# A selective-scan kernel: the D skip as accumulating transposes, the state copies on ScalarE, the gate on VectorE

## The reference

```python
xi = silu(conv(x @ in_proj_x));  z = x @ in_proj_z
dt, B, C = split(xi @ x_proj);   dt = softplus(dt @ dt_w + dt_b)
h[t] = exp(dt[t] * A) * h[t-1] + dt[t] * xi[t] * B[t]     # per channel and state
y[t] = sum over states of h[t] * C[t]
y    = (y + xi * D) * silu(z)
out  = y @ out_proj
```

## Time and profile before

| what | value |
|---|---|
| median of 3 runs | 5188.53 us (5188.35 to 5191.7) |
| the profiled execution: own time, span | 5190.08 us, 5188.0 us |
| Mamba loop, first scan to last | 162 to 3766 us |
| busy in the span: PE, DVE, ACT, POOL | 4402.9, 4073.9, 3191.4, 3548.5 us |
| busy between 160 and 3766 us: DVE, POOL, PE, ACT | 3545.0, 3438.7, 2967.1, 2551.0 us of 3606 |

### The profile page before, as it was taken

The page is one execution under the profiler, slowest core; times in us unless marked ns, Lnnn a source line. Parts: engine busy times, 40 slices in busy tenths (PEclk is TensorE's granted clock), DMA queues, the critical chain, the costliest instruction groups (busy, mean ns, idle before and its releaser), DMA issues. The chain is left out here.

```text
span 5188.0 us, 70665 instructions
## 1 busy us (share of the span) xinstructions
PE 4402.9 (85%) x22602; PEld 3147.1 (61%) x22602; DVE 4073.9 (79%) x4200; ACT 3191.4 (62%) x4771; POOL 3548.5 (68%) x2133
## 2 busy tenths in 40 slices
PE   3888888888888888888888888888679999999999
PEld 1455555555555555555555555555558888888887
DVE  4799999999999999999999999999933333333332
ACT  4767676776767777777677677767534443444343
POOL 5899999999999999999999999999910000000000
PEclk7899999999999999999999999999889999999999
DMA  4533232333223322232222223222230000000000
GB/s 144 184 115 101 99 106 98 115 103 103 100 99 105 104 103 100 105 111 103 105 94 102 107 104 112 102 104 94 81 114 17 9 17 9 17 9 17 9 17 9
DMA packets 152610, 433.73 MB, mean 84 GB/s; under 512 B 12352, under 2 KB 96704, under 8 KB 117568
## 3 DMA queue, kind: packets, MB, share of 16 engines
q1 hardware_dynamic: 151296, 416.96, 23.0%
q10 hardware_dynamic: 896, 11.54, 0.6%
HBM read 384.42 MB, written 55.57 MB: 85 GB/s over the span
## 5 line engine op out<-in xcount | busy, mean ns | idle before, releaser
L1011 POOL TENSOR_TENSOR m_dBx<-m_u,m_Bs 128x1024 f32<-128x1024 f32 x1024 | 2410.9, 2368 | 36.6 <-DVE m_h L1174 30.1
L1174 DVE TENSOR_TENSOR_SCAN m_h<-bank,m_state,m_dBx 128x512 f32<-128x512 f32 x1792 | 2192.0, 1263 | 46.4 <-ACT bank L895 43.7
L895 ACT ACTIVATE bank<-m_dt,cols 128x512 f32<-128x512 f32 x2048 | 1385.3, 690 | 869.3 <-DVE m_h L1174 848.0
L715 PEld LDWEIGHTS bank<-ident,m_h 128*128 128x128 f32 x8192 | 1019.5, 147 | 509.4 <-issue 358.2
L715 PE MATMUL bank<-ident,m_h 128*128 128x128 f32 x8192 | 1251.9, 283 | 81.6 <-DVE m_h L1183 68.8
L1183 DVE TENSOR_TENSOR m_h<-m_h,bank 128x1024 f32<-128x1024 f32 x896 | 1069.1, 1193 | 7.6 <-PE bank L697 7.5
L697 PE MATMUL bank<-ident,m_Ct 128*128 128x128 f32 x3584 | 596.4, 291 | 543.4 <-DVE m_h L1183 538.1
L697 PEld LDWEIGHTS bank<-ident,m_Ct 128*128 128x128 f32 x3584 | 396.5, 141 | 1041.6 <-DVE m_h L1183 928.1
L1446 POOL TENSOR_TENSOR mv<-mv,norm_c 128x4 f32<-128x4 f32 x16 | 3.2, 202 | 1226.9 <-DVE mv L1464 1226.9
L602 PE MATMUL bank<-m_hT,m_w_in 128*128 128x512 f32 x1024 | 545.8, 619 | 20.3 <-ACT m_hT L776 20.2
L602 PE MATMUL bank<-m_xpre,m_diag 128*128 128x512 f32 x1024 | 529.6, 602 | 0.0
(11 more groups left out here) (123 smaller groups left out, 5005.9 us busy)
## 6 DMA issues: line engine op xcount, KB each, us to landing
m_Bs<-b_dram SPq DMA_DIRECT2D x256, 1024.0 KB, 4.7
m_Cs<-c_dram SPq DMA_DIRECT2D x128, 256.0 KB, 4.5
m_xy<-in_x SPq DMA_DIRECT2D x16, 512.0 KB, 7.2
xn_dram<-m_xn SPq DMA_DIRECT2D x16, 512.0 KB, 6.9
x_dram<-m_base SPq DMA_DIRECT2D x16, 512.0 KB, 7.1
yb_dram<-m_ysb SPq DMA_DIRECT2D x16, 512.0 KB, 7.8
m_xn<-xn_dram SPq DMA_DIRECT2D x16, 512.0 KB, 3.8
m_xy<-yb_dram SPq DMA_DIRECT2D x16, 512.0 KB, 5.8
```

The costliest lines, as they stand in the source:

```text
L715: mm = pe.matmul(YB[b][:, o:o + P], h[:, k % NH, m, tok:tok + P], ident[:, :], start=(s == 0 and o == 0), stop=(s == DS - 1), is_transpose ...
L895: act.activation(DA[SLOT[k]][:, :], dt[:, ch.batch, m, :], ACT.Exp, scale=cols[:, ch.ps, col:col + 1]).then_inc(S["da"], 1)
L1011: pool.tensor_tensor(dBx[:, k % NDBX, :, :], u[:, ch.batch, m, :], Bs[:, k // BP % 2, k % BP, :].unsqueeze(1).broadcast_to((P, 2, T)), ALU ...
L1174: dve.tensor_tensor_scan(h[:, k % NH, m, flip(ch)], DA[SLOT[i]][:, flip(ch)], dBx[:, k % NDBX, m, flip(ch)], initial, ALU.mult, ALU.add).t ...
```

## The change

- The D skip moves: ScalarE computes xD = D * xi (`scale_skip`, new, at steps 14, 16, 18 and 20), and TensorE adds it to the sums in PSUM with 8 more accumulating transposes per half (`turn_skip`, new), behind the last `turn_h` of the half. The evacuation now waits for these (`y_turned`).
- `skip` on VectorE becomes `gate`: z = (turned sum in PSUM) * z. GpSimd's `gate` goes.
- `keep_state` goes from GpSimd to ScalarE, at steps 2, 6, 10 and so on to 62.
- `P_UNITS` has six units instead of four: 0, 6, 9, 14, 20, 25.
- The first pair of z's silus moves from step 14 to step 12.
- `xi` is held for one chunk instead of two, `acc` for one half instead of two; two more C rows are loaded per chunk, with the order of the loads on the SP queue changed.

```diff
-P_UNITS = (5, 10, 17, 21)
+P_UNITS = (0, 6, 9, 14, 20, 25)
...
-AT_XI, AT_ZS = (24, 24, 31, 31), (14, 14, 57, 57)
+AT_XI, AT_ZS = (24, 24, 31, 31), (12, 12, 57, 57)
...
-GATE_S = (28, 12)
+AT_XD = (14, 16, 18, 20)
...
@@ SP, body @@
                 load_b(ch, 2)
+                load_c(ch, 2)
                 load_b(ch, 3)
...
-                load_c(ch, 2)
+                load_c(ch, 3)
                 load_b(ch, 4)
+                load_c(ch, 4)
...
-                load_c(ch, 3)
                 load_b(ch, 5)
...
+                load_c(ch, 5)
...
@@ TensorE @@
+            def turn_skip(ch, half):
+                pe.wait_ge(S["skip"], ch.at(KI, 2 * half + 2))
+                for t in range(TS):
+                    for m in range(2):
+                        o = t % 2 * HW + m * P
+                        mm = pe.matmul(YB[t // 2][:, o:o + P], xD[:, 2 * half + m, t * P:(t + 1) * P], ident[:, :],
+                                       start=False, stop=True, is_transpose=True, skip_group_check=True)
+                mm.then_inc(S["y_turned"], 1)
...
                             turn_h(*done, b)
+                            if b == 1 and done[1] % DS == DS - 1:
+                                turn_skip(done[0], done[1] // DS)
...
@@ ScalarE @@
-                            wait(act, S["gate"], ch.at(2, -2))
+                            wait(act, S["u_ready"], ch.at(2, 0))
...
+            def scale_skip(ch, g):
+                for m in range(KI):
+                    if g == AT_XD[m]:
+                        if m == 0:
+                            act.wait_ge(S["xi"], ch.at(KI, KI))
+                            act.sem_inc(S["go"], 1)
+                            wait(act, S["y_turned"], ch.at(2, 0))
+                        col = COL_D + m
+                        act.activation(xD[:, m, :], xi[:, m, :], ACT.Copy, scale=cols[:, ch.ps, col:col + 1]
+                                       ).then_inc(S["skip"], 1)
+
+            def keep_state(ch, p):
+                k = 2 * p
+                act.wait_ge(S["scan"], ch.at(STEPS, 2 * k + 4))
+                act.copy(state[:, ch.batch, k:k + 2, :], h[:, k % NH:k % NH + 2, :, 0 if rev(ch) else T - 1]
+                         ).then_inc(S["save"], 1)
...
-                act.wait_ge(S["turned"], ch.at(NU, DS * (half + 1)))
+                act.wait_ge(S["y_turned"], ch.at(2, half + 1))
...
                     z_silu(ch, k)
+                    scale_skip(ch, k)
+                    if k % 4 == 2:
+                        old = unit(ch, (k - 6) // 2)
+                        if old:
+                            keep_state(old[0], old[1] // 2)
...
@@ GpSimd: gate and keep_state and their calls go @@
...
@@ VectorE @@
-            def skip(ch, g, m):
+            def gate(ch, g, m):
                 q = ch.batch
                 if g == AT_Y[m] + DVE_LAG:
-
+                    dve.wait_ge(S["z"], ch.at(KI, m + 1))
                     wait_filled(dve, ch, J_Y[m])
-                    dve.scalar_tensor_tensor(out=xi[:, q, m, :], in0=xi[:, q, m, :],
-                                             scalar=cols[:, ch.ps, COL_D + m:COL_D + m + 1],
-                                             in1=FB[BANK[J_Y[m]]][:, :],
-                                             op0=ALU.mult, op1=ALU.add).then_inc(drain[BANK[J_Y[m]]], 1)
+                    dve.tensor_tensor(z[:, q, m, :], FB[BANK[J_Y[m]]][:, :], z[:, q, m, :], ALU.mult
+                                      ).then_inc(drain[BANK[J_Y[m]]], 1)
```

More of the change, by code:

```diff
@@ L167 @@
     "sp_exp", "sp_ln", "dt_done", "u_ready", "b_st", "b_in0", "b_in1", "c_in0", "c_in1", "da", "dbx", "scan", "save",
-    "c_fill", "weigh_d", "weigh_p", "turned", "y_evac", "gate",
+    "c_fill", "weigh_d", "weigh_p", "turned", "skip", "y_turned", "y_evac",
     "y_out", "yb_in", "base_in", "base_out", "xn_in", "xn_out", "comb",
@@ L355, in mamba @@
         no_halo = sb("no_halo", [P, KI, HALO])
-        xi = sb("xi", [P, BATCH, KI, T])
+        xi = sb("xi", [P, KI, T])
+        xD = sb("xD", [P, KI, T])
         z = sb("z", [P, BATCH, KI, T])
@@ L647, in front @@
                         pe.wait_ge(S["xi"], ch.at(KI, m + 1))
-                        part(ch, J_B, m, KI, w_x[:, m, :], xi[:, q, m, :], B0 + 2 * DS)
+                        part(ch, J_B, m, KI, w_x[:, m, :], xi[:, m, :], B0 + 2 * DS)
                 if g == AT_C:
@@ L664, in turn_y @@
                     o = m % 2 * P
-                    turn(J_Y[m], lambda s: acc[:, half, s, o:o + P], ch)
+                    turn(J_Y[m], lambda s: acc[:, s, o:o + P], ch)
             def tail(ch, g):
@@ L677, in tail @@
                                     pe.wait_ge(S["w_out"], 16 * (ch.ps + 1))
-                                pe.wait_ge(S["gate"], ch.at(2, 2))
+                                wait_drained(pe, ch, J_Y[2])
                             wait_free(pe, ch, J_OUT[i])
@@ L715, in turn_h @@
                         mm = pe.matmul(YB[b][:, o:o + P], h[:, k % NH, m, tok:tok + P], ident[:, :],
-                                       start=(s == 0 and o == 0), stop=(s == DS - 1), is_transpose=True,
+                                       start=(s == 0 and o == 0), stop=False, is_transpose=True,
                                        skip_group_check=True)
@@ L747, in flush @@
                         turn_h(ch, NU + k - T_LAG, b)
+                turn_skip(ch, 1)
                 for g in range(STEPS):
@@ L829, in xi_silu @@
                         if m == 0:
-                            wait(act, S["gate"], ch.at(2, -2))
+                            wait(act, S["u_ready"], ch.at(2, 0))
                         wait_drained(act, ch, J_CONV[m])
-                        act.activation(xi[:, ch.batch, m, :], u[:, ch.batch, m, :], ACT.Silu).then_inc(S["xi"], 1)
+                        act.activation(xi[:, m, :], u[:, ch.batch, m, :], ACT.Silu).then_inc(S["xi"], 1)
+            def scale_skip(ch, g):
[13 more added lines that the diff above has]
+                         ).then_inc(S["save"], 1)
             def z_silu(ch, g):
@@ L842, in evacuate @@
             def evacuate(ch, half):
-                if has(ch, -1):
-                    wait_filled(act, ch.go(-1), J_Y[2 * half])
+                before = (ch, 0) if half else (ch.go(-1), 2) if has(ch, -1) else None
+                if before:
+                    wait_filled(act, before[0], J_Y[before[1]])
                     act.sem_inc(S["go"], 1)
-                    wait_filled(act, ch.go(-1), J_Y[2 * half + 1])
+                    wait_filled(act, before[0], J_Y[before[1] + 1])
                     act.sem_inc(S["go"], 1)
-                act.wait_ge(S["turned"], ch.at(NU, DS * (half + 1)))
+                act.wait_ge(S["y_turned"], ch.at(2, half + 1))
                 for b in range(2):
-                    act.copy(acc[:, half, 2 * b:2 * b + 2, :], YB[b][:, :].rearrange("p (t n) -> p t n", t=2)
+                    act.copy(acc[:, 2 * b:2 * b + 2, :], YB[b][:, :].rearrange("p (t n) -> p t n", t=2)
                              ).then_inc(S["y_evac"], 1)
@@ L982, in make_u @@
                 pool.wait_ge(S["dt_done"], ch.at(2, half + 1))
[L983 to L1000, removed]
+                pool.tensor_tensor(u[:, q, m, :], dt[:, q, m, :], xi[:, m, :], ALU.mult).then_inc(S["u_ready"], 1)
             def weigh_b(ch, k):
@@ L1062, in body @@
                     weigh_b(ch, k)
[L1063 to L1066, removed]
                     old = unit(ch, k - W_LAG)
@@ L1077, in body @@
                         add_dt(ch.go(1), 0)
[L1078 to L1081, removed]
                     if joins(ch, -2):
@@ L1191, in body @@
                             for i in (2, 3):
-                                skip(ch.go(-1), g, i)
+                                gate(ch.go(-1), g, i)
                         for i in range(2):
-                            skip(ch, g, i)
+                            gate(ch, g, i)
                     old = unit(ch, k - W_LAG)
```

6 lines of the change are left out of this document (2 added, 4 removed).

## The result

The changed kernel takes 5216.49 us (median of 5 runs, 5214.68 to 5218.46), the kernel before 5188.53 on the same chip (5 runs, 5187.05 to 5191.7). The ratio is 1.0053, with a 95% interval of 1.0038 to 1.0068. The forecast was no change, 5184, with a range of 5130 to 5230 that holds the result; on the main point, that the time would stay, the forecast was wrong.

The account below looks back on a forecast made before the run. VectorE, 98% busy in the Mamba loop, was taken as the bound. Its saved work and the changed waits summed to about 0.0 us per chunk; with first chunk and tail about -5 us, 5188.5 became 5184, range 5130 to 5230.

Parts of the forecast that it names:

- VectorE's work: Two C products fewer and four cheaper skips per chunk: -2.34 us per chunk, -75 us in all.
- the four spots: Steps 13, 25, 32 and 44 of a chunk, where ScalarE is late or nearly late for VectorE's scans.
- Scan 13: VectorE waits for ScalarE's decay behind the evacuation and the silus of z: +2.6 us per chunk.
- Scans 25, 32 and 44: VectorE's waits change per chunk by +0.6 us at scan 25, -0.6 at scan 32, -0.2 at scan 44.
- The first chunk and the tail: The first chunk, with no evacuation at step 11, gains 2 us; the tail after the last scan changes by -1.5.
- GpSimd's work: GpSimd's work per chunk falls by 3.1 us; its lead over VectorE shrinks but holds, so nothing was added.
- the rival of a dry GpSimd: GpSimd runs dry by 1 us or more per chunk, so VectorE waits for `dBx`: 5216 us, chance 0.05.
- Silus hidden: Rival: z's silus on ScalarE cost VectorE nothing, so the work alone counts: 5112 us, chance 0.17.
- the block of 5.15 us: On ScalarE, one decay, the silus of z with two table loads, and the next decay: 5.15 us from start to end.
- Slow transposes: Rival: TensorE's skip transposes cost 283 ns each rather than 110, delaying both evacuations: 5271 us, chance 0.14.
- Table switches: Rival: ScalarE's four D scalings each switch activation tables, 10.3 us per chunk: 5387 us, chance 0.04.
- the longer drain: Skill page's drain of about 1.38 us per ScalarE table switch; step 13 would wait 2.8 longer, some 5270; no chance given.

Follow-up runs that it names:

- run 1: The changed kernel with z's first silus back at step 14 and the D scalings at steps 16, 18, 20, 22: 5168.65 us.
- run 7: The changed kernel without the D skip on any engine (no D scalings, no skip transposes; y lacks D * xi): 5150.73 us.
- run 4: The changed kernel with GpSimd's old four units (5, 10, 17, 21) and the C loads to match: 5253.88 us.
- run 6: The changed kernel with the 512 KB load of x moved behind the third B load of the chunk: 5209.19 us.
- run 3: The kernel before the change, with only the 16 state copies per chunk moved to ScalarE: 5204.52 us.
- run 9: The changed kernel with the 128x4 variance step moved from VectorE to ScalarE, at its step 57: 5201.65 us.
- run 5: The changed kernel with the 128x4 variance step as scalar_tensor_tensor, epsilon from a tile, in place of tensor_scalar: 5215.61 us.

## Why the prediction was wrong

**VectorE's work and the four spots: right.** -75 was -78.5; the gate took 662 ns rather than 692. Scan 13 was +2.6 and waited 2.55, by the very mechanism (run 1 takes it away, run 7 takes 0.87 of it). Scans 25, 32 and 44 came as 0.57, none and 0.34, against 0.6, none and 0.45; run 4 gives the first two back with the units. Only scan 44 was mis-sized, -11.2 us in the place of -6, in the kernel's favour. Together the terms that the sum had come out at -12 us in the place of -3. The first chunk and the tail, -3.5 together, came as -5 behind the last scan and up to +3 ahead.

**The step that failed is the sum itself, at "GpSimd's work": "I take nothing".** I asked only whether VectorE would wait for `dBx`. It hardly does, 2.9 us in the loop: the rival of a dry GpSimd named 5216, nearly the measured time, but by a mechanism that is not there. Nor does it save the forecast that the result lies in its range: it lies there since -12 us of walked terms offset 40 us of terms that the sum didn't have. Two costs hang on when GpSimd works, a third stands at the pass switch, and none had a term:
- The loop's ends, +14.7: GpSimd's product for unit 25 comes at its unit 29, its last `dBx` is later, the burst of loads is later by as much, and the code behind it. Shown by run 6, which takes the whole of it away, by run 4, in which they are at 11.4 us with GpSimd's old units, and by run 3, which clears the longer code. I had walked one chunk and not the jump between two; the waits of 1 to 1.5 were in the trace of before, and the 1.4 of the earlier trace rows is one of them.
- The variance step, +17.7: shown by runs 3, 4 and 9 for its price, by runs 4 and 5 for what it waits on. Its 0.52 before was already three times its length beside an idle GpSimd.
- The pass switch, +7.5: first a wait of 3.1 for TensorE, then two gaps of issue (1.1 and 2.2), then 1.7 at scan 13. TensorE stands for 3.47 us there, and from 1873 to 1880 us its granted clock is 0.54, near its lower level of 1.2 GHz (0.98 in the 13 us ahead of that): the eight transposes of the skip, 1.04 us long in nearly every other group, take 1.92. It goes with the old units (run 4), and no run took it by itself. What starts it stays open. The rows of TensorE after:

```profile
1873.31 1.12 PE L719 MATMUL bank<-ident,m_h 128*128 128x128 f32 x4 [3.47 <-DVE m_h L1195]
1876.78 1.92 PE L731 MATMUL bank<-ident,m_xD 128*128 128x128 f32 x8
```

The Trainium skill, "SBUF — State Buffer" (SBUF: two separate sides), says that VectorE and GpSimd share a pair of ports by an exclusive lock, held for a whole instruction, for which VectorE asks in a two-port mode or with two SBUF inputs. The trace agrees with the page: both forms of the step end 0.02 to 0.03 us behind GpSimd's product, and the scans, the C products and the statistics steps, which have at most one SBUF tensor as input, don't wait. The second form has two SBUF inputs; whether the first runs in a two-port mode no run shows. I had not weighed it, since so small a step did not seem to matter.

**The rivals.** Silus hidden (5112): no, but at step 14 they nearly are, in the first pass; the block of 5.15 us must start two steps later. Slow transposes (5271): refuted by run 7, and by the 0.87 of the eight in the trace. Table switches (5387): no load stands by the scalings. The load of 1.28 is again followed by its activation 1.29 behind its start (1082.01 and 1083.30), so the longer drain that the prediction cites shows in neither trace.

**Chances.** Slower had 0.33, and of it only 0.05 for GpSimd. A part for what the one chunk could not show, the loop's ends and small steps of VectorE beside a fuller GpSimd, belonged in the sum: 10 ends at up to 2.4 (the growth now seen at one jump) and 15 steps at up to one product of 2.37 would have given a bound of +60.

## What to carry to other kernels

When an engine off the path is given other work, walk everything that is timed by it: the loads that its progress releases, what is queued behind these (code too, at a loop's jump), and every small step of the bound engine that runs beside it. Walk the jump between iterations as well as one iteration. When the consumer of a buffer moves, the order of the queue that fills it must move too.

## What was unexpected of the hardware

- A 128x4 step of VectorE, in two forms with all tensors in SBUF, takes 0.16 to 0.17 us beside an idle GpSimd, 1.42 when it comes early into a GpSimd product of 2.37, and up to 3.78. A statistics step as small keeps its 0.14 to 0.18.
- After a loop's jump ScalarE gets its code only when the data burst ahead of it is nearly through: a gap of 6.97 us where 2.1 MB end at 1059.6, 4.56 where they end at 1054.3 (the last activation ahead of the jump ends at 1054.90 and 1052.67), and 3.71, ended by a scan, with 512 KB out of the burst.
- Taking a stall from VectorE did not give its whole length back: 15 of 25 us, with 9 more in waits elsewhere (run 9).
